# A fused early-fusion transformer block on one core: prologue reordered, value groups copied by VectorE

## The reference, cut to what matters

```python
def reference(x, x_txt, ...):                       # x [8, 64, 256, 4], x_txt [8, 128]
    # token mixer (AFT): q, k, v by 64x64 weights with a bias each, per head
    ew = exp(w_bias * local_mask)                   # [256, 256]
    y = sigmoid(q) * (ew @ (exp(k) * v)) / (ew @ exp(k))
    h = layernorm(y @ out_w + out_b + flatten(x)) * ln_g + ln_b   # [8, 256, 256]
    h = concat([h, W_E[x_txt] * sqrt(256)])         # [8, 384, 256]
    # attention, 16 heads of 16, learned relative keys and values in a window of +-4
    h = h + attention(layernorm(h))
    # 8 experts of 256 hidden units, sigmoid router with zone and top-2 fallback
    h = h + sum_e w_e * (silu(n @ Wg_e) * (n @ Wu_e)) @ Wd_e,     n = layernorm(h)
    return h
```

## Time and profile before

| | us |
|---|---|
| median of 3 runs | 1249.13 (1246.06 to 1252.84) |
| profiled execution | 1249.12 |
| its span in the profile | 1247.3 |
| TensorE matmul busy | 1020.4 |
| VectorE busy | 753.0 |
| ScalarE busy | 451.2 |
| GpSimd busy | 247.8 |

### The profile page before, as it was taken

One profiled execution on the slowest core, in us unless ns is written; L12 is line 12 of the kernel. 1 busy time (PEld: TensorE's weight loads), 2 busy tenths in 40 slices (PEclk: granted clock), 3 DMA queues, 4 the chain that ended last, 5 costly groups with the idle time before them and its releaser, 6 DMA issues.

```text
span 1247.3 us, 16776 instructions
## 1 busy us (share of the span) xinstructions
PE 1020.4 (82%) x5668; PEld 744.4 (60%) x5668; DVE 753.0 (60%) x1597; ACT 451.2 (36%) x651; POOL 247.8 (20%) x262
## 2 busy tenths in 40 slices
PE   3536698888898798888898798988988888987798
PEld 2412277636786287745786377854876367862687
DVE  7347355774648755685658745685567746487343
ACT  1133512453124723355124622346224531347211
POOL 6228411021200402013200412004120212004000
PEclk9569789989999999999999999999999999999899
DMA  4286203602062110802044020722026020620100
GB/s 110 101 240 174 68 5 97 140 11 53 4 178 59 24 42 33 202 10 39 18 121 115 9 56 0 202 44 39 18 79 157 10 52 5 179 60 18 35 1 13
DMA packets 96962, 87.87 MB, mean 70 GB/s; under 512 B 67281, under 2 KB 85074, under 8 KB 95090
## 3 DMA queue, kind: packets, MB, share of 16 engines
q1 hardware_dynamic: 96524, 86.24, 28.3%
q0 software_dynamic: 384, 1.05, 0.3%
HBM read 60.35 MB, written 26.92 MB: 70 GB/s over the span
## 4 chain that ended last, share of the span: by engine, by line
PE 46%; issue 22%; DVE 17%; DMA 5%; ACT 4%; POOL 4%; SPq 2%; POOLq 0%; DVEq 0%; ACTq 0%
PE S L913 16%; PE S L934 8%; DVE maxima L1220 4%; PE S L844 4%; PE S L779 4%; PE S L827 4%; PE S L741 3%; DVE S L1241 3%; ACT scratch L1033 3%; PE S L658 1%; DMA txt_row<-in_L_txt_W_E,txt_idx 1%; DVE res L1374 1%; PE S L760 1%; SPq L566 1%; PE S L787 1%
## 5 line engine op out<-in xcount | busy, mean ns | idle before, releaser
L1491 POOL TENSOR_TENSOR bands<-scratch,one 64x432 f32<-64x432 f32 x128 | 119.1, 931 | 525.0 <-ACT scratch L1033 519.4
L1070 ACT ACTIVATE silu<-S 128x384 f32<-128x384 f32 x128 | 63.0, 492 | 352.2 <-PE S L913 243.6
L1220 DVE TENSOR_REDUCE maxima<-S 128x2 f32<-128x768 f32 x192 | 172.2, 951 | 19.0 <-PE S L787 17.6
L934 PE MATMUL S<-w_d,hT 128*128 128x256 f32 x768 | 182.0, 382 | 1.5 <-DVE hT L1362 0.7
L1241 DVE TENSOR_TENSOR S<-S,bands 64x144 f32<-64x144 f32 x384 | 154.3, 402 | 43.3 <-PE S L827 32.6
L1033 ACT ACTIVATE scratch<-S 128x768 f32<-128x768 f32 x192 | 154.8, 812 | 56.3 <-DVE S L1241 43.0
L779 PE MATMUL S<-k_st,q_st 128*128 128x384 bf16 x384 | 101.9, 334 | 68.0 <-DVE maxima L1220 39.7
L934 PEld LDWEIGHTS S<-w_d,hT 128*128 128x128 f32 x768 | 143.4, 191 | 22.2 <-issue 2.3
L1362 DVE TENSOR_TENSOR hT<-silu,S 128x384 f32<-128x384 f32 x128 | 70.7, 552 | 116.7 <-PE S L913 97.4
L827 PE MATMUL S<-q_st,k_st 128*128 128x384 bf16 x384 | 98.8, 356 | 40.2 <-ACT scratch L1033 36.7
L1011 ACT ACTIVATE scratch<-scratch 128x816 bf16<-128x816 bf16 x56 | 92.3, 1694 | 41.5 <-DMA scratch<-d_band_t 41.5
(11 more groups left out here) (167 smaller groups left out, 1515.6 us busy)
## 6 DMA issues: line engine op xcount, KB each, us to landing
bands<-d_band_s SPq DMA_DIRECT2D x16, 864.0 KB, 9.4
scratch<-d_band_t SPq DMA_DIRECT2D x8, 1632.0 KB, 9.6
d_parts<-scratch SPq DMA_DIRECT2D x48, 192.0 KB, 1.9
q_st<-d_parts SPq DMA_DIRECT2D x48, 192.0 KB
k_st<-d_parts SPq DMA_DIRECT2D x48, 192.0 KB
d_band_w<-bands SPq DMA_DIRECT2D x32, 240.0 KB, 3.9
out<-scratch SPq DMA_DIRECT2D x8, 384.0 KB, 2.6
x_in<-in_x SPq DMA_DIRECT2D x8, 256.0 KB, 3.6
```

Of the source, the lines that this page charges most:

```text
L934: mm = pe.matmul(D[:, i // 2, (i % 2) * E:(i % 2 + 1) * E], hT[:, (FT * e + m) % 3, i * P:(i + 1) * P], w_d[:, e, m, :], start=(m == 0), s ...
L1220: dve.tensor_reduce(dst, S[:, c0:c0 + 2, PAD:PAD + T], AX, ALU.max).then_inc(max_done.sem, 1)
L1491: nc.gpsimd.tensor_tensor(bands[rows, :, :, 2 * pair:2 * pair + 2].rearrange("p i w h -> p h i w"), win, one[rows].unsqueeze(2).unsqueeze( ...
```

## The change

The tokens and text indices of item 0 are issued ahead of group 0. The three bias rows leave group 0 and have a semaphore of their own, `bias_loaded`, for which TensorE's `mix_in` waits. The reordering transfers are issued behind group 1; group 2 no longer waits as a whole for them, but only its last three transfers, which are now the reordered columns, do. GpSimd clears `k_st` and `q_st` within `mix_sums` of round 0, behind the scaled text rows, and as f32 words. `prepare` is moved from behind `mix_out` to behind `turn_norm`; ScalarE's wait for `consts` moves to `project_qk`. The step `copy` is VectorE's in every round.

```diff
--- before.py
+++ after.py
@@ -71,7 +71,7 @@
 EPS = 1e-5
 ITEMS = AH * TT // 2
 WINS = P // BL
-N_LOADS = (9, 4, 10 + 3 + NJ)
+N_LOADS = (6, 4, 10 + 3 + NJ)
 N_ZERO = 6
 LAST_ROWS = 8
 N_CONSTS = 11
@@ -258,6 +258,7 @@
         ew_turned, ew_ready, resid_ready = sem("ew_turned"), sem("ew_ready"), sem("resid_ready")
         temp_inverse, wr_high, consts = sem("temp_inverse"), sem("wr_high"), sem("consts")
         row_mask, rows_ordered = sem("row_mask"), sem("rows_ordered")
+        bias_loaded = sem("bias_loaded")
         half_mask = sem("half_mask")
         gu_high, gu_low, pool_consts = sem("gu_high"), sem("gu_low"), sem("pool_consts")
         x_loaded = sig("x_loaded", 1, 16)
@@ -363,7 +364,7 @@
                 if name not in LATE_STEPS or ffn:
                     steps.append((name,))
                 fill(n)
-                if name == "mix_out" and not ffn:
+                if name == "turn_norm" and not ffn:
                     steps.append(("prepare",))
             if not ffn:
                 steps.append(("weights",))
@@ -459,9 +460,6 @@
                 (ident[:], a["ident"]),
                 (wkv[0:F, 0:F], a["tok_wk_t"]), (wkv[0:F, F:2 * F], a["tok_wv_t"]),
                 (wq_t[0:F, :], a["tok_wq_t"]),
-                (wkv[F:F + 1, 0:F], a["L0_tok_Wk_b"].unsqueeze(0)),
-                (wkv[F:F + 1, F:2 * F], a["L0_tok_Wv_b"].unsqueeze(0)),
-                (wq_t[F:F + 1, :], a["L0_tok_Wq_b"].unsqueeze(0)),
             ], [
                 (resid[F:F + 1, :, :], a["L0_tok_out_b"].rearrange("(o h c) -> o h c", o=1, h=H)),
                 (out_w[:], a["L0_tok_out_w"].rearrange("(k p) n -> p k n", p=P)),
@@ -481,26 +479,33 @@
             ]]
 
             emb_v = a["L0_attn_emb_rel_v"]
-            groups[2] += [(bq4[:], d_bias[0]), (bk1[:], d_bias[1]), (emb_k_rows, dram(d_emb, 0, (NJ, AD), (0, G8), (1, NJ)))]
             for j in range(NJ):
                 groups[2].append((emb_v_rows[HH * j:HH * (j + 1)], dram(emb_v, j * AD, (0, HH), (1, AD))))
+
+            groups[2] += [(bq4[:], d_bias[0]), (bk1[:], d_bias[1]),
+                          (emb_k_rows, dram(d_emb, 0, (NJ, AD), (0, G8), (1, NJ)))]
 
             def load(g):
                 assert len(groups[g]) == N_LOADS[g]
                 with nc.allow_non_contiguous_dma(reason="small bias and embedding columns, once"):
                     for n, (dst, src) in enumerate(groups[g]):
-                        if g == 0 and n == N_LOADS[0] - N_BIAS_ROWS:
-
-                            sp.wait_ge(rows_zero, 4)
+                        if g == 2 and n == N_LOADS[2] - 3:
+
+                            sp.wait_ge(rows_ordered, 3 * 16)
                         sp.dma_start(dst, src).then_inc(loaded[g], 16)
 
-            load(0)
-
-            with nc.allow_non_contiguous_dma(reason="small bias and embedding columns, once"):
-                for n, name in enumerate(("L0_attn_bq", "L0_attn_bk")):
-                    sp.dma_start(d_bias[n].rearrange("(d g) m -> d (g m)", d=AD),
-                                 a[name].rearrange("(h d) -> d h", d=AD)).then_inc(rows_ordered, 16)
-                sp.dma_start(d_emb, a["L0_attn_emb_rel_k"].rearrange("o j d -> d (o j)")).then_inc(rows_ordered, 16)
+            def bias_rows():
+                sp.wait_ge(rows_zero, 4)
+                for dst, src in ((wkv[F:F + 1, 0:F], a["L0_tok_Wk_b"]), (wkv[F:F + 1, F:2 * F], a["L0_tok_Wv_b"]),
+                                 (wq_t[F:F + 1, :], a["L0_tok_Wq_b"])):
+                    sp.dma_start(dst, src.unsqueeze(0)).then_inc(bias_loaded, 16)
+
+            def order_rows():
+                with nc.allow_non_contiguous_dma(reason="small bias and embedding columns, once"):
+                    for n, name in enumerate(("L0_attn_bq", "L0_attn_bk")):
+                        sp.dma_start(d_bias[n].rearrange("(d g) m -> d (g m)", d=AD),
+                                     a[name].rearrange("(h d) -> d h", d=AD)).then_inc(rows_ordered, 16)
+                    sp.dma_start(d_emb, a["L0_attn_emb_rel_k"].rearrange("o j d -> d (o j)")).then_inc(rows_ordered, 16)
 
             def load_x(b):
                 sp.dma_start(x_in[0:F, :, :], a["x"][b]).then_inc(x_loaded.sem, 16)
@@ -516,8 +521,10 @@
 
                 if not later(b):
                     load_x(b)
+                    load(0)
+                    bias_rows()
                     load(1)
-                    sp.wait_ge(rows_ordered, 3 * 16)
+                    order_rows()
                     load(2)
 
                     sp.wait_ge(zero_ready, 1)
@@ -669,6 +676,7 @@
             def mix_in(b):
                 if not later(b):
                     pe.wait_ge(ones_ready, 1)
+                    pe.wait_ge(bias_loaded, N_BIAS_ROWS * 16)
                     pe.wait_ge(ew_ready, 1)
                 pe.wait_ge(x_loaded.sem, x_loaded.at(b, 1))
 
@@ -970,8 +978,6 @@
                 nc.scalar.activation(wr_hi[:], w_r[:], ACT.Copy).then_inc(wr_high, 1)
 
             def turn_norm(b):
-                if not later(b):
-                    act.wait_ge(consts, N_CONSTS)
                 for k in range(KT):
                     act.wait_ge(xt_pe.sem, xt_pe.at(b, k + 1))
                     nc.scalar.activation(xn_t[:, k], S[:, k, 0:T], ACT.Copy).then_inc(xt_act.sem, 1)
@@ -979,6 +985,8 @@
             banks = [S[:, 2], S[:, 0], S[:, 1], O]
 
             def project_qk(b):
+                if not later(b):
+                    act.wait_ge(consts, N_CONSTS)
                 for n in range(4):
                     act.wait_ge(proj_pe.sem, proj_pe.at(b, n + 1))
                     dst, bias, scale = (qf, bq4, AD ** -0.5) if n < 2 else (kf, bk1, 1.0)
@@ -1032,10 +1040,6 @@
                 c0 = 2 * (n % 3)
                 nc.scalar.activation(dst, S[:, c0:c0 + 2, PAD:PAD + T], ACT.Exp).then_inc(exp_done.sem, 1)
 
-            def copy(b, g):
-                act.wait_ge(pv_done.sem, pv_done.at(b, g + 1))
-                nc.scalar.activation(o_sb[:, g], S[:, 6 + g % 2, 0:T], ACT.Copy).then_inc(o_copied.sem, 1)
-
             def turn_weights(b):
                 for g in range(KT):
                     act.wait_ge(rw_pe.sem, rw_pe.at(b, g + 1))
@@ -1071,7 +1075,7 @@
 
             rounds(act, {"mix_in": mix_in, "prepare": prepare, "turn_norm": turn_norm,
                          "project_qk": project_qk, "project_rel": project_rel, "maxima": maxima,
-                         "negate": negate, "attend": attend, "copy": copy, "turn_weights": turn_weights,
+                         "negate": negate, "attend": attend, "turn_weights": turn_weights,
                          "turn_attn": turn_attn, "turn_x2": turn_x2, "router": router, "gate": gate})
 
 
@@ -1240,6 +1244,10 @@
                             else bands[rows, 0:2, :, h])
                     dve.tensor_tensor(win, win, band, ALU.add).then_inc(sc_add.sem, 1)
 
+            def copy(b, g):
+                dve.wait_ge(pv_done.sem, pv_done.at(b, g + 1))
+                dve.tensor_copy(o_sb[:, g], S[:, 6 + g % 2, 0:T]).then_inc(o_copied.sem, 1)
+
             def turn_outputs(b):
 
                 dve.wait_ge(win_done.sem, win_done.at(b, WINS * 6))
@@ -1378,7 +1386,7 @@
             rounds(dve, {"mix_in": mix_in, "mix_sums": mix_sums, "mix_out": mix_out, "mix_norm": mix_norm,
                          "prepare": prepare, "norm_stats": norm_stats, "turn_norm": turn_norm,
                          "project_qk": project_qk, "project_v": project_v, "maxima": maxima,
-                         "negate": negate, "attend": attend, "turn_outputs": turn_outputs,
+                         "negate": negate, "attend": attend, "copy": copy, "turn_outputs": turn_outputs,
                          "turn_weights": turn_weights, "rel_values": rel_values, "residual": residual,
                          "turn_x2": turn_x2, "router": router, "router_zone": router_zone,
                          "router_rank": router_rank, "router_pick": router_pick,
@@ -1393,11 +1401,6 @@
                 nc.gpsimd.memset(dst[:], value).then_inc(pool_consts, 1)
             nc.gpsimd.memset(v_one[:], 1.0).then_inc(pool_consts, 1)
             pool.wait_ge(pool_consts, 5)
-            nc.gpsimd.memset(k_st[:], 0.0).then_inc(pool_consts, 1)
-            nc.gpsimd.memset(q_st[:], 0.0).then_inc(pool_consts, 1)
-            pool.wait_ge(pool_consts, 7)
-            nc.gpsimd.memset(k_st[0:NEG], 1.0).then_inc(pool_consts, 1)
-            pool.wait_ge(pool_consts, 8)
 
             def root(b, stats, steps, done, tiles):
 
@@ -1426,6 +1429,13 @@
                     pool.wait_ge(res_ready.sem, res_ready.at(b - 1, TT))
                 nc.gpsimd.tensor_tensor(hid[:, IT], txt_row[:], root_e[:].broadcast_to([P, E]), ALU.mult
                                         ).then_inc(hid_ready.sem, 1)
+                if not later(b):
+                    for st in (k_st, q_st):
+                        nc.gpsimd.memset(st[:].rearrange("p h t -> p (h t)").bitcast(F32), 0.0
```

(4 more changed lines are left out.)

## The result

The changed kernel takes 1258.08 us, median of 8 runs (1257.06 to 1260.26), against 1249.26 us before (8 runs); the ratio is 1.0065, with a 95% interval of 1.0044 to 1.0086. It is slower, by about 8 us, where I had said faster by 4.8. In a second series of runs it came out at 1.0120 (1.0096 to 1.0144). Medians and ratios here leave out executions that took over 1.5% longer than the fastest of the same kernel.

The account below looks back on a forecast made before the run. The prediction took an unbroken chain of waits to bound the prologue and mostly TensorE the middle rounds. Its terms, -8.1 + 0.4 + 2.9 = -4.8 us, gave 1244.3 us from 1249.13, range 1240 to 1250.

Parts of the forecast that it names:

- Part 1, tokens first: Prologue: tokens issued first and a shorter mask cast start TensorE at 11.4 in place of 19.48, 8.1 us gained.
- Part 2, the stacks: Prologue: GpSimd's later clears, 2.6 us each, cost nothing under cover if VectorE's `resid` copies come before them.
- the rival of the clears: Prologue: `resid` copies stand behind GpSimd's memsets, first product with `ek` 2.6 to 8 us late, 1247 to 1252; chance 15%.
- Part 3, the constants: Round 0, before q and k: 1.6 us gained, 2.0 lost by colliding with GpSimd's `bo_all` addition; 0.4 us lost.
- the clock rival: Round 0's output product: TensorE's clock doesn't fall, 1242.3 (chance 13%), or it rises later after the start, 1246.3.
- Part 4, the copies: Attention of every round: group copies on VectorE delay window adds, 0.42 us a round, 2.9 us lost in all.
- the slower rival: Attention: each group copy waits for GpSimd's window copies, 19 to 41 us over 24 copies, 1263 to 1285; chance 5%.
- The free copy: Attention: a copy costs 0.35 us or less, or else the constants don't collide, 1241.4 to 1243.0; chance 12%.
- the hidden prologue: Prologue: expert loads hold GpSimd's splits at a fixed time, so only the 2.9 lost remains, 1252; chance 5%.
- the estimate of 0.53 us: Group copy on VectorE: 120 + 384 cycles by the Trainium skill; if all occupied VectorE, 1.6 us more, 1245.9.

Follow-up runs that it names:

- the repeated run: The changed kernel unaltered, run again on the same chip as its separated parts: 1261.06 us, 1.0120 against the kernel before.
- e11_stacks_early: The prologue alone, but with the stacks cleared at the start again, as bf16: 1246.77 us, 1.0006 against the kernel before.
- the copies alone: The kernel before with only the group copies moved from ScalarE to VectorE: 1264.09 us, 1.0147 against the kernel before.
- e6_small_ops_on_dve: The prologue alone, with VectorE waiting and clearing one column at each group copy's place, copies staying on ScalarE: 1251.91 us, 1.0034 against the kernel before.
- the prologue alone: The changed kernel with the group copies back on ScalarE: 1240.49 us, 0.9954 against the kernel before.

## Why the prediction was wrong

*Part 1, tokens first: right.* 8.1 us forecast, 8.3 measured; the first product starts at 11.18 (11.4 forecast), held by `ew_t`.

*Part 2, the stacks: right in the execution of the result, by luck.* Nothing waited for GpSimd there; the clears took 2.65 us each, as halved, and the text row was scaled at 8.98, late enough for VectorE's `resid` copies to pass (8.32 to 8.80, the first clear at 9.53). It was close, by 0.7 us, and in the repeated run the rival of the clears came true: with the text row at 8.18, 7.7 of the 8.6 us were lost again. I gave it 15%; two of eleven profiles have the full loss. That the clears had held the cast and the `resid` copies in the kernel before is shown by `e11_stacks_early`.

*Part 3, the constants: right.* 0.4 lost forecast, 0.5 measured; 0.9 gained without the collision forecast and measured. By the Trainium skill (SBUF — State Buffer, "SBUF: two separate sides") an operation of VectorE with two SBUF inputs waits for a GpSimd operation that reads SBUF; the trace agrees, with 1.77 against 0.38 us, the 1.77 ending 0.2 us behind GpSimd's addition (40.66 + 1.81).

By the start of q and k the gain was 8.6 where 7.7 was forecast; the rest is mostly the output product, part of which ran at the high level of the clock, a part of the clock rival.

*Part 4, the copies: wrong, and this decided the sign.* The term was 2.9 us, and the whole stood at 1244.3, at most 1250; the copies alone cost 18, and the time was 1258.08. The step failed in three places.
1. The price. I took 0.46 us from a 384-element operation on PSUM and the start of its successor. That successor read SBUF. Before window adds, which read and write PSUM, the copy takes 0.59, the upper bound of my range (0.6). In the trace the add starts 0.03 us behind the copy's end, while the operation on SBUF of the earlier trace rows starts 0.08 before its predecessor's. Per copy it is 0.2 more than the 5.92 us between groups, in place of 0.12, and with the fourth some 0.7 a round in place of 0.42: 6 us in eight rounds.
2. I costed only the engine's time of the new instructions, not their place in the stream. Eight more instructions a round on VectorE (four waits, four copies) moved a fetch by 1 us, into the transfer of the band tile, which then lands up to 0.8 later. The cover was 0.1 us wide, so VectorE's first operation on the tile came 0.7 us later in each of six rounds: 4 us. Eight short instructions a round in the copies' place cost 10 us in `e6_small_ops_on_dve`: some 3 of them before the tile's first use, and the others where TensorE was at its lower level.
3. I took a round's growth as the sum of what is put in. 1.48 us put in cost 2.9, and TensorE was at its lower clock level for longer, 10.2 us a round against 5.8 in the prologue alone (rounds 1 to 6). The half of this that I did have, the clock rival, looked at round 0 alone. The 145 us that I took for a middle round had such a stretch more than the rounds 3 to 6, which take 143.4.

*The rivals.* The copy never waited for GpSimd (all are about 0.56 us long), so the slower rival had the wrong mechanism, though its threshold, 0.2 us a copy, was about what the direct price came to. The free copy fell (0.59 against 0.35), and so did the hidden prologue: 122.67 became 113.32. The clears did meet the copies, in other executions. The copy's length, 0.56, was near the estimate of 0.53 us, but by that term too, 1245.9, the kernel would have been faster.

In the two profiles of the result, the six rounds 1 to 6 divide their 15.5 us into 4 for price, 4 for the late tile and 7 for the clock. That the 7 us lie where TensorE was at its lower level is in the traces; that the other two terms bring the clock down there is argued and not shown, for no run holds the clock and moves the copies. How the 18 us of the medians divide is not settled beyond that. Nor was it tried why the adds start 0.13 us later behind a copy than an operation on SBUF does.

## What to carry to other kernels

Price a moved instruction by the row of an operation followed by the same kind of successor on the same engine, and multiply by the rounds before comparing with a gain in the prologue. In a loop whose transfers have no slack, look at where the instruction fetches fall, and count a delay on the path as worth up to twice its length, as here. Keep VectorE's copies between SBUF tiles and its two-input operations away from long GpSimd operations, by a semaphore and not by 0.7 us of luck: one profile doesn't show what the next execution does.

## What was not expected of the hardware

A 1632 KB transfer landed up to 0.8 us later (9.6 to 10.4) in 20 of 30 rounds in which an instruction fetch of some 0.01 MB came 8.0 to 8.9 us after its issue, and in none of 54 others. TensorE's granted clock fell 1.5 us behind 18 matmul instructions of 8 columns, with TensorE without a pause, in some rounds and not in others; a round's length then moves by more than what is put in (143.4 to 146.8 us for 1.48). The text row of item 0 was ready for GpSimd at 8.2 us in one execution of a kernel and at 9.0 in another, and with it 7.7 us of the start of q and k came or went.
